# Attention probabilities split in fp16 halves and turned by a transposing DMA instead of TensorE

## Chip, core and metric

One NeuronCore of a Trainium2 chip runs the whole kernel as one program. The metric is the device time of one execution in microseconds (us). Engines: PE (TensorE: matmul and transpose into PSUM), DVE (VectorE), ACT (ScalarE), POOL (GpSimd), SP (SyncE, which here only issues DMAs). Each engine works through its own instructions in order and waits on semaphores.

## What is computed

One cross-attention layer and one FFN with 4-bit block quantisation, fp32 in and out. x is 2 x 1024 rows of 256, the context 2 x 154 rows of 256.

```python
# x = x + attention(layernorm(x), ctx, ctx);  16 heads of 64
q = einsum('bnd,hdk->bhnk', layernorm(x), proj_q) + bias_q
k = einsum('bnd,hdk->bhnk', ctx, proj_k) + bias_k
v = einsum('bnd,hdv->bhnv', ctx, proj_v) + bias_v
attn = softmax(q @ k.T / sqrt(64))            # rows of 154 per head
x = x + concat_heads(attn @ v) @ w_out.T
# x = x + ffn(layernorm(x));  fp4(.): blocks of 16, absolute maximum / 6 as scale, rounded to the grid 0 .. 6
h = silu(fp4(xn) @ fp4(w_gate).T) * (fp4(xn) @ fp4(w_up).T)     # 704 wide
x = x + fp4(h) @ fp4(w_down).T
```

## The kernel before

Every fp32 product is made of three fp16 matmuls: each operand is held as a high half and a low half (value minus high half), and `three` (L396) adds high x high, high x low and low x high in PSUM. The high half is made by ACT, the low half by DVE, as a rule out of PSUM.

After the loads and the keys, attention runs in 8 steps `i` of 256 rows (two tiles `s` of 128 rows). Sixteen heads are handled in four quads `j`, so there are 64 quads in all. For a quad, `score` (L522) puts 4 x 154 columns into two PSUM banks, `row_max` (L994, DVE) takes the maxima, `exps` (L742, ACT) the exponentials with their sums into `prob`, `inverse` (L1001, DVE) the reciprocal and `norm` (L1233, POOL) multiplies by it: the first 128 columns of each head in place, the other 26 into `rests`. The probabilities must then be turned, since the product with v sums over the 154 context rows. `turn_p` (L538, PE) transposes them as fp32 against the identity in five groups of four 128x128 blocks for each tile (four quads, and one group that gathers the rests), into one of two PSUM banks. `p_high` (L753, ACT) and `p_low` (L1005, DVE) write the halves of each group into `pT`, which has two buffers by step.

The four `heads` (L470) of step i-1, the four `query` parts (L507) of step i+1 and the projection `project` (L487) of step i-1 run among the groups of step i. Heads, the first values and the output weights share one PSUM bank (`O_BANK`, in the order `O_ORDER`, L253) with the projection, and query parts and the turned x another (`Q_BANK`). `add_attention` (L1010) adds the projection to x. In steps 1 to 6 a sixth of the FFN weights is quantised in passing: `block_scales` and `minus_grid` on DVE, `value` and a rounding product on POOL, an absolute value on ACT.

The body `attention` of each engine has ten groups a step (five to a tile), and runs the exponentials one tile ahead of the turning. The quantised FFN weights are turned (`turn_weights`, L547) in the last half step, when all exponentials are done. Then 16 FFN tiles follow (`ffn`), whose first four tiles also hold three of the four heads of step 7 and its projection. Stores are SP's only DMAs after the loads.

Of the kernel before, what the change touches and what calls it, by code (L numbers as in the profile page):

```python
# [33 lines left out]
CHUNKS = H + QUADS  # L34
GROUPS = QUADS + 1
# [6 lines left out]
W_STEPS = 6  # L42
WSLICE = WALL // W_STEPS

# [53 lines left out]
def xattn_ffn_kernel(nc, x, ctx_in, proj_q, bias_q, proj_k, bias_k, proj_v, bias_v, w_out,  # L98
                     w_gate, w_up, w_down, out):
    with ExitStack() as ctx:  # L100
# [16 lines left out]
        pT = sb("pT", [P, 2, 2, CHUNKS, 2 * P], F16)  # L117
# [22 lines left out]
        A2 = KC * W1 + FC * D + 2 * FP_ + 2 * FP_ + F + 6 * D  # L140
# [14 lines left out]
        bv = pT[0:1, 1].rearrange("p a c n -> p (a c n)")[:, 0:4 * H * DK].bitcast(F32)  # L155
# [4 lines left out]
        prob = arena[:, RAW:RAW + 2 * SC].rearrange("p (s n) -> p s n", s=2)  # L160
        REST0 = RAW + 2 * SC
        rests = arena[:, REST0:REST0 + 2 * H * RESTP].rearrange("p (s h n) -> p s h n", s=2, h=H)
        assert REST0 + 2 * H * RESTP <= 4 * RAW
# [15 lines left out]
        w1_h, w1_l = (take(KC * W1 // 2).bitcast(F16).rearrange("p (c n) -> p c n", c=KC) for _ in range(2))  # L179
        wdT = take(FC * D).bitcast(F16).rearrange("p (c n) -> p c n", c=FC)  # L180
        hq = take(2 * FP_).rearrange("p (s n) -> p s n", s=2)
        hT_h, hT_l = (take(FP_).bitcast(F16).rearrange("p (s n) -> p s n", s=2) for _ in range(2))
        silu = take(F)
# [4 lines left out]
        def over(n):  # L188
            mark[0] += n
            assert mark[0] <= 6 * RAW  # L190
            return arena[:, mark[0] - n:mark[0]]

        x_tmp = tuple(over(2 * D) for _ in range(3))
        assert mark[0] <= RAW + SC
        hid = over(2 * F).rearrange("p (s n) -> p s n", s=2)
        h_tmp = [tuple(over(F) for _ in range(3)), (over(F), wtmp[0], wtmp[1])]
        assert mark[0] <= 4 * RAW
        y = take(2 * D).rearrange("p (s n) -> p s n", s=2)
        xq = take(2 * D).rearrange("p (s n) -> p s n", s=2)
        xnorm = take(2 * D).rearrange("p (s n) -> p s n", s=2)  # L200
# [8 lines left out]
        T_BANK, O_BANK, Q_BANK = 4, 6, 7  # L209
# [14 lines left out]
        xn_ready, xt_mm, xt_high, xt_low = sem("xn_ready"), sem("xt_mm"), sem("xt_high"), sem("xt_low")  # L224
        q_mm, q_high, q_low = sem("q_mm"), sem("q_high"), sem("q_low")
        scored, max_done = sem("scored"), sem("max_done")
        exp_done, rinv_ready, normed = sem("exp_done"), sem("rinv_ready"), sem("normed")
        pt_mm, pt_high, pt_low = sem("pt_mm"), sem("pt_high"), sem("pt_low")
        o_mm, o_high, o_done = sem("o_mm"), sem("o_high"), sem("o_done")
# [4 lines left out]
        wt_mm, wt_high, wt_low, pad2_zero = sem("wt_mm"), sem("wt_high"), sem("wt_low"), sem("pad2_zero")  # L234
# [18 lines left out]
        O_ORDER = [("wo", n) for n in range(PAIRS // 2)]  # L253
        O_ORDER += [("v", b, n) for b in range(B) for n in range(3)]
        O_ORDER += [(kind, i, j) for i in range(STEPS) for kind, n in (("pv", QUADS), ("proj", 1)) for j in range(n)]
        O_AT = {j: n for n, j in enumerate(O_ORDER)}
        O_HIGH_AT = {j: n for n, j in enumerate(j for j in O_ORDER if j[0] != "proj")}
# [4 lines left out]
        def jobs_of(g):  # L262

            return range(W1_JOBS * g // GROUPS, W1_JOBS * (g + 1) // GROUPS)

        def down_jobs(s):

            return (range(W1_JOBS, len(WT_JOBS) - 1), range(len(WT_JOBS) - 1, len(WT_JOBS)))[s]

        def wt_bank(n):  # L270

            return n % 4 if n < W1_JOBS else HT_BANK + n % 2
# [15 lines left out]

        LAST_HEADS = (None, (0, 0), (0, 1), (1, 0))
        HEADS = ((0, 1), (0, 3), (1, 0), (1, 2))  # L290

        def queries(i):

            return ((0, 3), (0, 4), (1, 0), (1, 1)) if i == 0 else ((0, 0), (0, 2), (0, 4), (1, 1))

        def rows_in(i, s, g):

            if i == 0 and (s, g) == (0, 2): return 1
            return i + 2 if (s, g) == (1, 4) and exists(i + 2) else None

        def q_bank(i, j):

            return O_BANK + j % 2 if i == 0 else Q_BANK
# [18 lines left out]
        def last_quad(g):  # L322

            return min(QUADS - 1, g)

# [7 lines left out]
        def quad_T(part, i, s, g):  # L333

            return pT[:, i % 2, part, 4 * g:4 * g + 4, s * P:(s + 1) * P]

        def of_o(job):

            kind, a, j = job
            o = ps[:, O_BANK, :]  # L340
            if kind == "v":
                return o, v_h[:, a, j * 512:(j + 1) * 512], v_l[:, a, j * 512:(j + 1) * 512]
            return o, both(hidT_h[:, 2 * j:2 * j + 2]), both(hidT_l[:, 2 * j:2 * j + 2])
# [7 lines left out]
        def _(sp):  # L351
# [29 lines left out]
            sp.dma_start(wd_tiles, w_down.rearrange("(r p) f -> p r f", p=P)).then_inc(ld_ffn, 16)  # L381

# [12 lines left out]
        def _(pe):  # L395
# [34 lines left out]
            def next_o(job):  # L430

                wait(pe, o_done, O_AT[job])
                return ps[:, O_BANK, :]

            def turn_o(n):
                if n == 0: pe.wait_ge(ld_o, 16)
                wo = raw["o"].rearrange("p (r n) -> p r n", r=KC)
                o = next_o(("wo", n))
# [4 lines left out]
                last.then_inc(o_mm, 1)  # L443

            def values(b, n):
                o = next_o(("v", b, n))
# [4 lines left out]
                pe.matmul(o, ones[:, :], bv_l[:, n * 512:(n + 1) * 512], start=False, stop=True).then_inc(o_mm, 1)  # L451

            def rest_values(b):
                o = next_o(("v", b, 2))[:, 0:QUADS * DK].rearrange("p (a k) -> p a k", a=QUADS)
# [13 lines left out]
                last.then_inc(o_mm, 1)  # L468

            def heads(i, j):  # L470

                b = batch(i)
                if j == 0: pe.wait_ge(pt_low, GROUPS * (2 * i + 2))
                o = next_o(("pv", i, j))
                parts = ((v_h, vl_h, 0), (v_l, vl_l, 0), (v_h, vl_h, 1))
                for k in range(2):
                    for n, (vh, vr, part) in enumerate(parts):
                        for u in range(2):
                            h = 4 * j + 2 * k + u
                            pe.matmul(o[u * DK:(u + 1) * DK, k * 256:(k + 1) * 256], vh[:, b, h * DK:(h + 1) * DK],  # L480
                                      pT[:, i % 2, part, h], start=n == 0, stop=False)
                        for u in range(2):
                            last = pe.matmul(o[u * DK:(u + 1) * DK, k * 256:(k + 1) * 256], vr[:, b, j, 2 * k + u],
                                             pT[:, i % 2, part, H + j], start=False, stop=n == 2)
                last.then_inc(o_mm, 1)

            def project(i, part):  # L487
                if part == 0:
                    pe.wait_ge(o_done, O_AT[("pv", i, QUADS - 1)] + 1)
                    next_o(("proj", i, 0))  # L490
                todo = [(s, p) for s in range(2) for p in range(PAIRS)]
                for s, p in todo[16 * part // 3:16 * (part + 1) // 3]:
                    last = three(ps[:, O_BANK, s * D:(s + 1) * D], hidT_h[:, p, s * P:(s + 1) * P],
                                 hidT_l[:, p, s * P:(s + 1) * P], wot_h[:, p], wot_l[:, p], p == 0, p == PAIRS - 1)
                if part == 2: last.then_inc(o_mm, 1)

            def turn_x(i):

                pe.wait_ge(xn_ready, i + 1)
                wait(pe, q_low, QUADS * i)  # L500
                v = xn.rearrange("p s (d c) -> p s c d", c=KC)
                for c in range(KC):
                    for s in range(B):
                        last = pe.transpose(ps[:, Q_BANK, (2 * c + s) * P:(2 * c + s + 1) * P], v[:, s, c], ident[:, :])
                last.then_inc(xt_mm, 1)

            def query(i, j):  # L507

                if j == 0:
                    pe.wait_ge(xt_low, i + 1)  # L510
                elif q_bank(i, j) == q_bank(i, j - 1):
                    pe.wait_ge(q_low, QUADS * i + j)
                else:
                    wait(pe, q_low, j - 1)
                for k in range(2):
                    p = 2 * j + k
                    for c in range(KC):
                        last = three(ps[:, q_bank(i, j), k * 256:(k + 1) * 256], wq_h[:, c, p * P:(p + 1) * P],
                                     wq_l[:, c, p * P:(p + 1) * P], xnT_h[:, c], xnT_l[:, c], c == 0, c == KC - 1)
                last.then_inc(q_mm, 1)  # L520

            def score(i, s, j):  # L522


                n = QUADS * (2 * i + s) + j
                if s == 0:
                    pe.wait_ge(q_low, QUADS * i + j + 1)
                wait(pe, exp_done, n - 1)
# [9 lines left out]
            def turn_p(i, s, g):  # L538
                pe.wait_ge(normed, QUADS * (2 * i + s) + last_quad(g) + 1)
                wait(pe, pt_low, GROUPS * (2 * i + s) + g - 1)  # L540
                for k in range(4):
                    h = 4 * g + k
                    v = prob[:, s, h * L:h * L + P] if g < QUADS else rests[:, s, 4 * k:4 * k + 4].rearrange("p h n -> p (h n)")
# [3 lines left out]
            def turn_weights(jobs):  # L547

                for n in jobs:
                    kind, c, j0 = WT_JOBS[n]  # L550
                    if n == 0:
                        pe.wait_ge(wq_done, W_STEPS)
# [770 lines left out]
```

## Time and profile before

| | us |
|---|---|
| median of 3 runs | 435.87 |
| lowest and highest of the runs | 433.01, 435.90 |
| span of the profiled execution, first to last instruction | 431.8 |
| one attention step in the middle, by the repeat of the chain | 28.54 |
| first `hidden` (L1148) of the FFN | at 287.90 |

The profile is of one execution. Its busy times count an engine as busy while any instruction runs; matmuls overlap, and so do ACT's instructions, so a group's count times its mean can exceed its busy time. The chain of waits is followed back from the last instruction; its pieces show which engine ended each stretch. The span leaves out what lies before the first and after the last instruction, so it is compared with a run only roughly.

### The profile page before, as it was taken

Reading aid. Unit: us, or ns where it says so; the run is one execution under the profiler, and the core shown is the slowest. Engines: PE = TensorE matmul, PEld = TensorE weight load, DVE = VectorE, ACT = ScalarE, POOL = GpSimd, SP = SyncE. Lnnn points to the kernel's source line nnn. Section 1 sums busy time; section 2 is a strip of 40 time slices with the busy share of each in tenths; the row PEclk is TensorE's granted clock in tenths of the full one; section 3 lists DMA queues with packets and bytes.
Section 4 is the critical chain, followed back from the end, with each engine's and each line's share of the span. In section 5 each row is a group of like instructions: output and inputs, shape, how many; then the busy total and the mean of one; then the engine's idle time right before and its main releaser. Section 6 shows DMA issues by size and latency. Waiting matters only on the chain.

```text
span 431.8 us, 9502 instructions
## 1 busy us (share of the span) xinstructions
PE 367.8 (85%) x3691; PEld 282.7 (65%) x3691; DVE 348.9 (81%) x676; ACT 276.8 (64%) x869; POOL 200.1 (46%) x235
## 2 busy tenths in 40 slices
PE   1864798999989989999899967988785999999985
PEld 1543664777868778778687755855563776777764
DVE  2989866996988969879889798569779799999692
ACT  4766979887997897879978775365142255433331
POOL 3455313354454543544545544026643657676710
PEclk9998699999999999999999997999899799999999
DMA  7970000000000000000000000000000000000001
GB/s 218 322 275 1 2 2 0 5 2 0 4 2 2 0 4 2 1 2 4 2 2 2 2 1 2 0 2 2 1 2 13 14 20 18 14 24 14 24 27 36
DMA packets 8445, 11.48 MB, mean 27 GB/s; under 512 B 524, under 2 KB 6352, under 8 KB 8401
## 3 DMA queue, kind: packets, MB, share of 16 engines
q1 hardware_dynamic: 8401, 10.88, 8.0%
q8 instruction: 29, 0.48, 0.5%
q14 instruction: 15, 0.12, 0.1%
HBM read 8.78 MB, written 2.10 MB: 25 GB/s over the span
## 4 chain that ended last, share of the span: by engine, by line
DVE 38%; ACT 28%; PE 28%; issue 3%; DMA 1%; POOL 0%; SPq 0%; DVEq 0%; ACTq 0%
ACT arena L747 14%; PE ps L398 7%; PE ps L400 7%; PE ps L399 7%; ACT arena L738 5%; ACT pT L756 4%; DVE arena L1058 4%; DVE negmax L998 4%; DVE arena L1056 3%; DVE arena L989 3%; DVE arena L1182 2%; DVE pT L1007 2%; PE ps L544 2%; DVE blk_h L1023 2%; DVE arena L1148 2%
## 5 line engine op out<-in xcount | busy, mean ns | idle before, releaser
L747 ACT ACTIVATE arena<-ps,negmax 128x154 f32<-128x154 f32 x256 | 98.4, 430 | 16.1 <-DVE negmax L998 16.0
L1238 POOL TENSOR_TENSOR arena<-arena,rinv 128x104 f32<-128x104 f32 x64 | 23.1, 361 | 114.9 <-DVE rinv L1003 114.9
L1239 POOL TENSOR_TENSOR arena<-arena,rinv 128x512 f32<-128x512 f32 x64 | 66.7, 1042 | 0.0
L1007 DVE TENSOR_TENSOR pT<-ps,pT 128x512 f16<-128x512 f32 x80 | 54.6, 682 | 13.0 <-ACT pT L756 13.0
L747 ACT ACTIVATION_READ_ACCUMULATOR arena<-ps,negmax 128x1 f32 x256 | 63.4, 248 | 0.0
L544 PE MATMUL ps<-ident,arena 128*128 128x128 f32 x320 | 53.7, 292 | 4.0 <-DVE pT L1007 4.0
L756 ACT ACTIVATE pT<-ps 128x512 f16<-128x512 f32 x80 | 51.5, 644 | 5.5 <-PE ps L544 5.4
L998 DVE TENSOR_REDUCE negmax<-ps 128x4 f32<-128x616 f32 x64 | 50.2, 785 | 0.3 <-PE ps L534 0.2
L534 PE MATMUL ps<-kT_h,arena 64*128 64x154 f16 x512 | 37.8, 233 | 12.7 <-ACT arena L747 12.0
L398 PE MATMUL ps<-arena,xnT_h 128*128 128x352 f16 x128 | 40.8, 319 | 8.5 <-DVE xnT_l L1066 6.7
L544 PEld LDWEIGHTS ps<-ident,arena 128*128 128x128 f32 x320 | 35.2, 145 | 14.9 <-issue 7.9
L398 PE MATMUL ps<-arena 128*128 128x256 f16 (+2 forms) x120 | 35.6, 297 | 8.0 <-DVE arena L902 5.8
L534 PEld LDWEIGHTS ps<-kT_h,arena 64*128 64x128 f16 x512 | 23.2, 95 | 26.8 <-issue 17.1
L400 PE MATMUL ps<-arena,xnT_l 128*128 128x352 f16 x128 | 40.8, 318 | 0.0
L399 PE MATMUL ps<-arena,xnT_h 128*128 128x352 f16 x128 | 40.7, 318 | 0.0
L839 ACT ACTIVATE arena<-ps 128x704 f32<-128x704 f32 x16 | 12.1, 757 | 43.3 <-PE ps L400 43.3
L738 ACT ACTIVATE arena<-ps,biasT 128x256 f16<-128x256 f32 x64 | 27.6, 498 | 17.4 <-PE ps L400 17.4
L398 PE MATMUL ps<-wot_h,arena 128*128 128x256 f16 x128 | 34.9, 272 | 3.9 <-DVE arena L960 3.9
L398 PE MATMUL ps<-xnT_h,wq_h 128*128 128x256 f16 x128 | 35.0, 274 | 3.1 <-POOL wq_l L1230 1.7
L480 PE MATMUL ps<-pT,v_h 128*64 128x256 f16 x256 | 35.0, 283 | 1.2 <-DVE xs L1014 1.2
L399 PE MATMUL ps<-arena 128*128 128x256 f16 (+2 forms) x120 | 35.5, 296 | 0.0
L400 PE MATMUL ps<-arena 128*128 128x256 f16 (+2 forms) x120 | 35.5, 295 | 0.0
(153 smaller groups left out, 1039.3 us busy)
## 6 DMA issues: line engine op xcount, KB each, us to landing
out_dram<-arena SPq DMA_DIRECT2D x16, 128.0 KB, 1.7
xs<-in_x_dram SPq DMA_DIRECT2D x2, 512.0 KB, 7.3
arena<-in_L_xattn_w_out_dram SPq DMA_DIRECT2D x1, 1024.0 KB, 11.9
xs<-in_x_dram SPq DMA_DIRECT2D x2, 384.0 KB, 6.7
wffn<-in_L_ffn_w_down_dram SPq DMA_DIRECT2D x1, 704.0 KB, 9.3
wffn<-in_L_ffn_w_gate_dram SPq DMA_DIRECT2D x1, 640.0 KB, 7.7
wffn<-in_L_ffn_w_up_dram SPq DMA_DIRECT2D x1, 640.0 KB, 8.3
arena<-in_ctx_dram SPq DMA_DIRECT2D x1, 308.0 KB
```

Source lines behind the costliest of these rows:

```text
L398: pe.matmul(o, a_h, b_h, start=start, stop=False)
L399: pe.matmul(o, a_h, b_l, start=False, stop=False)
L400: return pe.matmul(o, a_l, b_h, start=False, stop=stop)
L480: pe.matmul(o[u * DK:(u + 1) * DK, k * 256:(k + 1) * 256], vh[:, b, h * DK:(h + 1) * DK], pT[:, i % 2, part, h], start=n == 0, stop=False)
L534: last = pe.matmul(ps[:, 2 * (j % 2) + u, k * L:(k + 1) * L], q[r, p, s * P:(s + 1) * P], kt[r, batch(i), p], start=n == 0, stop=n == 2)
L544: last = pe.transpose(ps[:, T_BANK + (s + g) % 2, k * P:(k + 1) * P], v, ident[:, :])
L738: last = act.activation(q_h[:, 2 * j + k], ps[:, q_bank(i, j), k * 256:(k + 1) * 256], ACT.Identity, bias=biasT[:, 2 * j + k:2 * j + k + 1])
L747: last = act.activation(prob[:, s, h * L:(h + 1) * L], ps[:, 2 * (j % 2) + k % 2, (k // 2) * L:(k // 2 + 1) * L], ACT.Exp, bias=negmax[:, ...
L756: act.activation(quad_T(0, i, s, g), ps[:, T_BANK + (s + g) % 2, :].rearrange("p (c n) -> p c n", c=4), ACT.Copy).then_inc(pt_high, 1)
L998: dve.tensor_reduce(negmax[:, s, 4 * j:4 * j + 4].rearrange("p (k u) -> p u k", k=2), v, AX.X, ALU.max, negate=True).then_inc(max_done, 1)
L1007: dve.tensor_tensor(quad_T(1, i, s, g), ps[:, T_BANK + (s + g) % 2, :].rearrange("p (c n) -> p c n", c=4), quad_T(0, i, s, g), ALU.subtrac ...
L1239: pool.tensor_tensor(v[:, :, 0:P], v[:, :, 0:P], r.to_broadcast([P, 4, P]), ALU.mult).then_inc(normed, 1)
```

## The change

`turn_p`, `p_high` and `p_low` out of PSUM go. POOL's `norm` writes the normalised quad to a new tile `normal` of 5 x 128 columns (four heads of 128, and the four rests of 26 padded to 32 each). `high_p` copies it to fp16, on ACT for odd quads and on DVE for even ones; `low_p` subtracts, on DVE for three quads of eight and on POOL for five. Both halves stand side by side in `split` (four buffers, one per quad `j`), and one transposing DMA per quad, issued by SP, turns all ten 128x128 blocks of it into `pT`. The loops of all engines become 64 slots, one per quad, with `score`, maximum and exponentials of quad n, `norm` of n-1 and the halves of n-2. Everything else that goes through PSUM (turned x, query parts, heads, values, output and FFN weights) becomes a task with a place in one order, `TASKS`, over three banks instead of two. The projection gets a bank of its own and is done by one pair of heads in each slot. The turns of the gate and up weights move into slots 57 to 62, next to the last exponentials; `layernorm` for the FFN covers five steps first and three later, instead of six and two. `prob` has one buffer per quad instead of two tiles. The heads of step 7 come in the first two FFN tiles, its projection in tiles 1 to 3.

```diff
+        def heads_at(i, j):
+            return 8 * (i + 1) + (2, 3, 5, 7)[j]
+        def query_at(i, j):
+            return 8 * (i - 1) + ((5, 6, 7, 8) if i == 1 else (4, 6, 8, 9))[j]
+        def wt_at(n):
+            return (57, 57, 60, 60, 62, 62)[n]
+        def task_bank(n):
+            if n == 0: return 7
+            if n <= QUADS: return 6 + (n - 1) % 2
+            return (4, 5, 7)[n % 3] if n < BODY else 4 + n % 2
+        def high_by_act(n):
+            return n % 2 == 1
+        def low_by_dve(n):
+            return n % 8 in (2, 5, 6)
...
+            def turn_p(n):                                   # SP
+                i, s, j = place(n)
+                wait_low(sp, n)
+                if i == 1: sp.wait_ge(task_mm, TASK_AT[VALUES[-1]] + 1)
+                if i >= 2: sp.wait_ge(task_mm, TASK_AT[("h", i - 2, j)] + 1)
+                sp.dma_start_transpose(pT[:, i % 2, j, :, :, s * P:(s + 1) * P].rearrange("p a c n -> p (a c) n"),
+                                       split[:, j]).then_inc(turned[j], 16)
...
+            for n in range(SLOTS):                           # PE
+                score(n)
+                if parts_of(n): project(*parts_of(n))
+                for t in tasks_of(n):
+                    task(t)
...
+            def high_p(n):                                   # ACT; DVE has the same with tensor_copy
+                j = n % QUADS
+                act.wait_ge(normed, n + 1)
+                wait(act, turned[j], 16 * (n // QUADS))
+                act.activation(part_of(j, 0), normal[:, j], ACT.Copy).then_inc(high_act, 1)
...
+            def slot(n):                                     # DVE, without the FFN's parts
+                row_max(n)
+                if n >= 1: inverse(n - 1)
+                if n >= 2 and not high_by_act(n - 2): high_p(n - 2)
+                if n >= 1:
+                    for t in tasks_of(n - 1):
+                        low(t)
+                if n >= 2 and low_by_dve(n - 2): low_p(n - 2)
+                if i == 0: first(n)
+                if m == 3 and i >= 2: add_attention(i - 2)
...
+            def low_p(n):                                    # POOL; DVE has the same
+                j = n % QUADS
+                wait_high(pool, n)
+                pool.tensor_tensor(part_of(j, 1), normal[:, j], part_of(j, 0), ALU.subtract).then_inc(low_pool, 1)
...
-            def turn_p(i, s, g):                             # PE
-                pe.wait_ge(normed, QUADS * (2 * i + s) + last_quad(g) + 1)
-                wait(pe, pt_low, GROUPS * (2 * i + s) + g - 1)
-                for k in range(4):
...
-                    last = pe.transpose(ps[:, T_BANK + (s + g) % 2, k * P:(k + 1) * P], v, ident[:, :])
-                last.then_inc(pt_mm, 1)
```

## Rows read from the trace of the kernel before

**Rows 1.** The page's first part: busy time, share of the span, instructions.

```profile
span 431.8 us, 9502 instructions
PE 367.8 (85%) x3691; PEld 282.7 (65%) x3691; DVE 348.9 (81%) x676; ACT 276.8 (64%) x869; POOL 200.1 (46%) x235
```

**Rows 2.** Windows: from:to and length, then busy us of each engine.

```profile
core 0: us, PE busy (x) PEld busy (x) DVE busy (x) ACT busy (x) POOL busy (x), PEclk, DMA share, GB/s
137.24:165.78 28.54, 26.85 (x334) 21.89 (x332) 23.88 (x47) 24.20 (x91) 13.87 (x19) 1.00 0.01 2
```

**Rows 3.** Chain of waits in that step: start us, us, engine and line.

```profile
138.72 0.49 ACT pT L756
139.70 1.49 ACT arena L747 x8
157.99 0.44 PE ps L544 x4
161.04 0.59 PE ps L544 x4
```

**Rows 4.** Single lines: durations min/median/max in ns; then groups: busy us, mean ns.

```profile
L1007 DVE TENSOR_TENSOR pT<-ps,pT x80: 628/691/693, 43.6 to 274.7; 128x512 f16<-128x512 f32 x80
L998 DVE TENSOR_REDUCE negmax<-ps 128x4 f32<-128x616 f32 x64 | 50.2, 785 | 0.3 <-PE ps L534 0.2
L955 DVE TENSOR_TENSOR vl_l<-ps,vl_h 26x256 f16<-26x256 f32 x8 | 3.4, 420 | 1.3 <-ACT vl_h L728 1.2
```

**Rows 5.** Groups by shape: nearest rows to the new operations out of SBUF.

```profile
L1230 POOL TENSOR_TENSOR arena<-arena 128x1024 f16<-128x1024 f32 x2 | 4.2, 2126 | 2.3 <-ACT arena L683 2.3
L777 ACT ACTIVATE arena<-arena 128x704 f32<-128x704 f32 x15 | 11.8, 786 | 0.0
L782 ACT ACTIVATE arena<-arena 128x512 f32<-128x512 f32 x8 | 5.0, 630 | 2.6 <-POOL arena L1246 2.6
L1177 DVE TENSOR_TENSOR arena<-arena 128x704 f32<-128x704 f32 x1 | 0.9, 893 | 0.0
L1174 DVE TENSOR_SCALAR arena<-arena 128x704 f32<-128x704 f32 x1 | 0.5, 527 | 0.0
L907 DVE BATCH_NORM_STATS2 stats<-xs 128x6 f32<-128x256 f32 x32 | 11.7, 414 | 0.3
```

**Rows 6.** Timelines of DVE and POOL (start us, us), and a line's undisturbed duration.

```profile
260.75 1.04 POOL L1239 TENSOR_TENSOR arena<-arena,rinv 128x512 f32<-128x512 f32 x1
260.93 0.88 DVE L938 SCALAR_TENSOR_TENSOR ln<-ln 128x12 f32<-128x12 f32 x1
261.85 0.17 DVE L939 TENSOR_TENSOR ln<-ln 128x12 f32<-128x12 f32 x1
...
297.61 2.23 POOL L1246 TENSOR_TENSOR arena<-arena,blk_h 128x704 f32<-128x704 f32 x1
297.71 0.87 DVE L1056 SCALAR_TENSOR_TENSOR arena<-arena 128x704 f32<-128x704 f32 x1
298.62 1.96 DVE L1058 SCALAR_TENSOR_TENSOR arena<-arena 128x704 f32<-128x704 f32 x1
...
L1246 POOL TENSOR_TENSOR arena<-wffn,blk_w x6: 1385/1387/1389, 91.9 to 234.6; 128x704 f32<-128x704 f32 x6
```

**Rows 7.** Windows of L747 alone (ACT busy, records); then of DVE's layernorm tile.

```profile
80.00:251.40 171.40, 80.31 (x392) 1.00 0.01 2
251.40:262.00 10.60, 4.78 (x24) 1.00 0.01 2
...
30.00:47.00 17.00, 5.57 (x19) 1.10 (x2) 0.78 0.00 0
251.00:262.50 11.50, 4.84 (x19) 0.03 (x1) 1.00 0.01 2
```

**Rows 8.** Chain of waits from the last exponential to the FFN.

```profile
260.17 0.18 DVE rinv L1003
287.90 0.81 DVE arena L1148
```

**Rows 9.** The page: GB/s in 40 slices; a DMA issue, KB, us to landing.

```profile
GB/s 218 322 275 1 2 2 0 5 2 0 4 2 2 0 4 2 1 2 4 2 2 2 2 1 2 0 2 2 1 2 13 14 20 18 14 24 14 24 27 36
out_dram<-arena SPq DMA_DIRECT2D x16, 128.0 KB, 1.7
```

More of the change, by code:

```diff
@@ L589, in first_o, with task @@
+            def task(t):
+                if t[0] == "x": turn_x(t[1])
+                if t[0] == "q": query(t[1], t[2])
+                if t[0] == "h": heads(t[1], t[2])
+                if t[0] == "w": turn_weights(t[1])
+                if t[0] == "wo": turn_o(t[1])
+                if t[0] == "v":
+                    if t == VALUES[0]:
                         pe.wait_ge(w_low, 3)
@@ new lines, in weights_high @@
+            def weights_high(n):
+                kind, c, j0 = WT_JOBS[n]
+                o = task_out(("w", n))
+                if kind == "w1":
+                    w = min(4, W1T - j0) * P
+                    last = act.activation(w1_h[:, c, j0 * P:j0 * P + w], o[:, 0:w], ACT.Copy, scale=-FS)
+                else:
+                    act.wait_ge(pad2_zero, 1)
+                    for k in range(2):
+                        m = min(P, F - (j0 + k) * P)
+                        last = act.activation(wdT[0:m, j0 + k, 0:D], o[0:m, k * D:(k + 1) * D], ACT.Copy, scale=-FS)
+                last.then_inc(task_high, 1)
@@ L831, in _ @@
+            act.wait_ge(w_scaled, 1)
+            split_part("v", wv_h, 1.0, 0)
+            high(("q", 0, 0))
+            split_part("v", wv_h, 1.0, 1)
+            for j in range(1, QUADS):
+                high(("q", 0, j))
             act.activation(unused[:, 0:1], biasT[:, 0:1], ACT.Exp)
-            for j in range(QUADS):
-                exps(0, 0, j)
             act.wait_ge(pad_zero, 3)
-            steps(act, attention)
+            for n in range(SLOTS):
+                slot(n)
+            if high_by_act(SLOTS - 2): high_p(SLOTS - 2)
@@ L1106, in stats_of @@
+            low(("x", 0))
             def stats_of(i):
@@ L1277, in _, with slot @@
-            steps(pool, attention, last=W_STEPS)
-            value_x(0)
+            def slot(n):
+                i, m = divmod(n, 8)
+                w = i - 1 if 0 < i <= W_STEPS else None
+                if n >= 1: norm(n - 1)
+                if n >= 2 and not low_by_dve(n - 2): low_p(n - 2)
+                if n == 16:
+                    pool.wait_ge(task_mm, TASK_AT[VALUES[-1]] + 1)
+                    pool.memset(wdT[:, FC - 1, :].bitcast(F32), 0.0).then_inc(pad2_zero, 1)
+                if w is not None:
+                    if m == 2:
+                        value(wtmp[0], wffn[:, w * WSLICE:(w + 1) * WSLICE], [blk_w[:, r] for r in range(4)],
+                              wscaled, wlowered, wvalued, w)
+                    if m == 7:
+                        pool.wait_ge(wgrid, w + 1)
+                        pool.tensor_tensor(blocks(wffn[:, w * WSLICE:(w + 1) * WSLICE]), blocks(wtmp[0]), spread(blk_w[:, 1]),
+                                           ALU.mult).then_inc(wq_done, 1)
+                if n == 60: value_x(0)
@@ L1279, in _ @@
+            for n in range(SLOTS):
+                slot(n)
+            norm(SLOTS - 1)
+            for n in (SLOTS - 2, SLOTS - 1):
+                if not low_by_dve(n): low_p(n)
             round_x(0)
```

665 lines of the change are left out of this document (312 added, 353 removed).

## The prediction

> **What bounds the kernel now.** I read the page's shares first: TensorE is busy for 85% of a span of 431.8 us [rows 1]. An average over stages says little, so next the windows: in one attention step of 28.54 us TensorE has 26.85, ACT 24.20, DVE 23.88 and POOL 13.87 us of work [rows 2]. The reader should see three engines near the limit and one half empty. The chain of waits inside that step hands over between them: ACT's exponentials (1.49 us for a quad of heads) and its copy of turned probabilities (0.49) in the first half, TensorE's matmuls and transposes (0.44 to 0.59 for four) in the second [rows 3]. Last the count of exponentials by window: 392 + 24 records after 80 us, eight to a quad, so 52 of 64 quads remain at 80 us. The last ends just before the reciprocal at 260.17, and the first FFN product (L1148) comes at 287.90, 27.7 us later, after turns, copies and projections that stand alone there [rows 7, 8]. So there are three things to gain: the first 80 us, the period, and that 27.7 us.
>
> **The change, part by part.** All per step of eight slots.
>
> *TensorE* loses ten groups of four fp32 transposes, about 0.5 us each [rows 3]: 26.85 - 5 = 21.9 us. Heads, queries and projection are the same matmuls, spread one task and one pair to a slot.
>
> *ACT* loses ten copies of 0.49 [rows 3] and gains four high halves of 128x640 from SBUF. The row for 704 is 0.786 and for 512 0.630 [rows 5], so 0.73: 24.2 - 4.9 + 2.9 = 22.2 us.
>
> *DVE* loses ten low halves of 0.68 [rows 4]. It gains four copies of 640 (one-source SBUF op, 704 in 0.527 [rows 5], so 0.49) and three subtractions of 640 (704 in 0.893 [rows 5], so 0.82): 23.9 - 6.8 + 2.0 + 2.5 = 21.6 us.
>
> *POOL* keeps its normalisation and gains five subtractions of 640. POOL's own fp32-minus-fp16 row has 1024 in 2.126 [rows 5], so 1.33: 13.9 + 6.6 = 20.5 us.
>
> By busy time alone all four engines come to 20.5 to 22.2 us. Before, period over the busiest engine was 28.54/26.85 = 1.06, which would make 23.5 to 24.5 us.
>
> *But DVE and POOL do not run freely beside each other.* At 260.93 DVE starts an operation on 12 columns that needs 0.17 us elsewhere and takes 0.88: it ends at 261.81, with POOL's 1.04 us multiplication from 260.75. At 297.61 POOL's 704-wide multiplication takes 2.23 us instead of 1.39, and DVE's from 298.62 takes 1.96 instead of 0.89 [rows 6]. The three there need 0.87 + 0.89 (another 704-wide one of two inputs, [rows 5]) + 1.39 = 3.15 us and get 2.97 from first start to last end: they ran in turn. Operations of DVE that read PSUM show no such stretch: the 80 low halves stay at 0.68 [rows 4]. The change takes DVE's second reading from PSUM to SBUF and gives POOL a second one as well. Work that excludes itself per step: POOL 20.5, DVE's halves 4.5, its two FFN-weight operations 1.8, in all 26.8 us. A period cannot be much shorter if the copies are excluded too, and 24.8 if they are not (no row shows a copy beside POOL). DVE is in order, so each of its nine such operations waits for what POOL has running: POOL is on for about three quarters of the time with operations of about 1.1 us, so some 0.45 us each, 4 us a step, and DVE stands at 21.6 + 4 = 25.6 before any hand-over. With 1.06 for hand-overs that is 27.2; I take 27.5, with 24.5 and 30 as ends.
>
> The Trainium skill (SBUF — State Buffer, Who interferes with whom) states this as an exclusive lock for a whole operation: DVE takes it with two SBUF inputs or in its fast copy mode, POOL whenever it reads SBUF. The rows above agree for two inputs; by the rule the copies are locked as well, the 26.8 case.
>
> *The DMA* turns 128x1280 fp16, 327,680 bytes, once a slot. No row shows a transposing DMA. From below: the loads moved 322 GB/s in the second slice, so 1.02 us. From above: ten 128x128 blocks, each as slow as a 128 KB store from issue to landing, 1.7 us [rows 9], in turn: 17 us. I take the first end plus one landing, about 2.7 us, since a store of similar form streams its rows in one landing. SP issues it alone and has nothing else to do before the first store. It is covered: by 3.4 us of slot for its rate, and by about four slots between the low half (slot n+2) and the heads (n+6) for its latency. Without that cover heads wait, then projection, then the buffer of four quads, which stalls the high halves.
>
> *Start and step 0.* Slot 0's maximum follows the last query half, so about 31.5 us. DVE in slots 0 to 7: eight maxima of 0.785, reciprocals 1.4, value halves 4x0.68 + 8x0.42, one turned x and one output-weight half 1.4, two query parts 1.9, six statistics 2.5, normalisation steps 5.6 [rows 4, 5, 7], probability halves 3.1: 28 us, with waits for POOL 29.5. Slots 0 to 7 end at 61; before, 12 quads stood at 80 us, now 61 + 5.5 slots of 3.44, so 13.5. Worth 5 us.
>
> *Steps 1 to 6:* 6 x 27.5 = 165, to 226. *Step 7* has the weights' turns and a normalisation with 19 dependent small operations; on DVE maxima 6.3, reciprocals 1.4, halves 4.4, head halves 2.7, weight halves 3.8, add and statistics 1.5, normalisation 4.8 [rows 7], x quantisation 2.8: 27.7, with waits for POOL 30.5. Last exponential at 257.
>
> *Tail.* The weights' turns and most of the projection are done in slots. From the last exponential: reciprocal and normalisation 1.6, high half 0.7, POOL's low half 1.3, rounding x 1.1, two turns and halves 1.6, four projection pairs 2.6, gate and up 3.6, silu 0.8, hand-overs 0.8: 14 us, to 271, against 287.9. The last DMA has those 14 us as cover. Two head tasks move into each of the first two FFN tiles, where three and the projection stood before: I leave the rest of 143.9 us as it is.
>
> *Sum:* 271 + 143.9 = 415 for a span of 431.8, a gain of 17. The median of the runs shown is 435.87 with 433.01 the lowest, so 1 to 4 us lie around the span; with 2, **417 us**. Where it goes: start 5, last exponential earlier by 3 in all (steps 1 to 6 gain, step 7 gives back), tail 14.
>
> **Rivals.** *The engines do not collide:* period 24.5 and no added waits in steps 0 and 7: 417 - 18 - 4 = 395. For it: the four busy sums; against it: the rows of operations in turn.
>
> *The DMA sets the pace* (the other side). A transfer of T us binds from 3.4 us on; the last exponential then stands at about 41 + 60T and the time at that + 160. It is level with before at T = 3.9 us (84 GB/s), 2% slower at 4.05, and at 17 us the time is 1,220. For it: nothing shows this kind of transfer. Against it: plain ones reach 322 GB/s. The Trainium skill gives both sides. VectorE: DVE Perf Modes (The three transpose paths) has 1.309 us for one 128x128 block against 0.390 on TensorE; ten in turn would be 13 us, and 41 + 60x13 + 160 = 980, an estimate. DMA: Bandwidth & Descriptors (Latency and other measured facts) has 261 GB/s for a transposing DMA, so 1.26 us, and the change would stand. No run here shows either.
>
> *Nothing gained in the steps:* waits for POOL add up along the in-order queues to a period of 30 to 30.5, 417 + 15 to 18 = 432 to 435: the same. For it: DVE's wait is on the way of every maximum, hence of every exponential.
>
> **How the numbers follow.** Forecast (period 26 to 29) 0.48, 406 to 427; no collisions 0.20, 390 to 403; DMA-paced 0.22, of which a quarter below 450; nothing gained 0.10. From 390 to 445 holds 0.48 + 0.20 + 0.10 + 0.03, about 8 in 10. One per cent is about what a measurement of this kernel can tell from no change. Faster: 0.48 + 0.20, less a little: 0.67. Same: 0.10. Slower: 0.23.
>
> **What would show it.** Right: attention periods of 26 to 29 us with DVE's 640-wide halves well above 0.49 and 0.82 on average, POOL's above 1.33, a DMA under 3.4 us a slot, and 14 us from last exponential to first L1148's counterpart. Wrong: periods of 24 with those at their bare durations; or SP's transfers back to back, with high halves waiting for them.

## The result and the profile after

The changed kernel takes 431.44 us (median of 11 runs, 429.8 to 432.14) against 434.68 for the kernel before beside it: a ratio of 0.9927, 95% interval [0.99, 0.9953]. That is 0.7% faster, inside the 1% that the prediction called no change, where it had put 417 us. Its chances stood on faster (0.67), with 0.10 on this outcome. The span went from 431.8 to 427.9 us.

The page's first part, to be held against [rows 1]:

```profile
span 427.9 us, 9077 instructions
PE 337.4 (79%) x3371; PEld 250.3 (58%) x3371; DVE 363.5 (85%) x652; ACT 259.6 (61%) x821; POOL 273.2 (64%) x275
```

The work moved as planned: TensorE lost 30 us, ACT 17, POOL gained 73. DVE, which was to lose 2.3 us a step by its bare operations, *gained* 15 in all and is now the busiest engine. Windows by the prediction's own terms (from:to and length, then busy us of each engine), cut at the maxima of slots 0, 8, 48 and 56, at 267.90, where the last record of the exponentials starts, and at the first FFN product (L1204 here):

```profile
31.67:67.21 35.54, 25.52 (x241) 13.41 (x242) 25.30 (x65) 24.16 (x90) 15.40 (x18) 0.81 0.24 47
67.21:205.64 138.43, 114.30 (x1450) 89.23 (x1450) 130.06 (x219) 110.83 (x420) 113.88 (x120) 0.95 0.52 94
205.64:239.73 34.09, 25.35 (x311) 19.42 (x311) 32.80 (x60) 22.77 (x87) 25.50 (x26) 0.91 0.49 91
239.73:267.90 28.17, 22.02 (x239) 16.41 (x237) 23.17 (x48) 21.93 (x84) 19.45 (x22) 0.80 0.41 79
267.90:288.70 20.80, 11.98 (x100) 8.83 (x100) 8.83 (x17) 6.74 (x14) 7.47 (x8) 0.75 0.33 64
288.70:427.90 139.20, 121.79 (x916) 91.19 (x912) 122.30 (x193) 55.51 (x103) 77.43 (x65) 0.99 0.05 16
```

| term | forecast | measured |
|---|---|---|
| maximum of slot 0 | 31.5 | 31.7 |
| slots 0 to 7 (step 0) | 29.5 | 35.5 |
| steps 1 to 5 | 5 x 27.5 = 137.5 | 138.4 |
| step 6 | 27.5 | 34.1 |
| step 7, to the last exponential | 30.5 | 28.2 |
| tail, to the first FFN product | 14 | 20.8 |
| the rest of the FFN | 143.9 | 139.2 |

The measured terms add up to 427.9. The period of a plain step was right to 1%; three terms of some 6 to 7 us each were not. Read against before, by the last record of the exponentials (first before, then after; start us, us):

```profile
259.59 0.21 ACT L747 ACTIVATION_READ_ACCUMULATOR arena<-ps,negmax 128x1 f32 x1
267.90 0.29 ACT L805 ACTIVATION_READ_ACCUMULATOR arena<-ps,negmax 128x1 f32 x1
```

The exponentials end 8.4 us *later* (268.2 for 259.8), and what follows them is 12.3 us shorter (159.7 for 172.0).

### The profile page after: what moved, and what is told of

Same layout as the page of the kernel before. It is cut to its first block, busy times and chain, and to the rows that moved or that the text cites. A ratio compares the mean times of both kernels' runs of the same rounds, so it can differ in the third digit from the quotient of the medians.

```text
span 427.9 us, 9077 instructions
## 1 busy us (share of the span) xinstructions
PE 337.4 (79%) x3371; PEld 250.3 (58%) x3371; DVE 363.5 (85%) x652; ACT 259.6 (61%) x821; POOL 273.2 (64%) x275
## 2 busy tenths in 40 slices
DMA packets 92413, 32.44 MB, mean 76 GB/s; under 512 B 84492, under 2 KB 90320, under 8 KB 92369
## 4 chain that ended last, share of the span: by engine, by line
DVE 58%; PE 18%; POOL 14%; issue 5%; ACT 3%; DMA 1%; SPq 0%; DVEq 0%; POOLq 0%
DVE negmax L1036 6%; POOL arena L1304 5%; POOL arena L1298 5%; DVE arena L1049 5%; DVE arena L1055 4%; DVE arena L1112 4%; DVE arena L1114 4%; DVE arena L998 3%; PE ps L456 3%; PE ps L458 3%; PE ps L591 3%; PE ps L457 3%; DVE arena L1027 3%; DVE arena L1238 3%; DVE blk_h L1069 2%
## 5 line engine op out<-in xcount | busy, mean ns | idle before, releaser
L805 ACT ACTIVATE arena<-ps,negmax 128x154 f32<-128x154 f32 x256 | 96.5, 395 | 46.8 <-DVE negmax L1036 46.5
L1297 POOL TENSOR_TENSOR arena<-arena,rinv 128x104 f32<-128x104 f32 x64 | 30.1, 470 | 64.5 <-DVE rinv L1042 64.5
L1298 POOL TENSOR_TENSOR arena<-arena,rinv 128x512 f32<-128x512 f32 x64 | 70.5, 1102 | 0.0
L1304 POOL TENSOR_TENSOR arena<-arena 128x640 f16<-128x640 f32 x40 | 63.7, 1592 | 0.8 <-ACT arena L816 0.8
L591 PE MATMUL ps<-kT_h,arena 64*128 64x154 f16 x512 | 39.8, 241 | 28.6 <-DVE arena L1027 18.7
L805 ACT ACTIVATION_READ_ACCUMULATOR arena<-ps,negmax 128x1 f32 x256 | 53.8, 210 | 0.0
L554 PE MATMUL ps<-wot_h,arena 128*128 128x256 f16 x128 | 37.8, 295 | 1.0 <-DVE arena L998 0.3
L555 PE MATMUL ps<-wot_l,arena 128*128 128x256 f16 x128 | 37.5, 293 | 0.0
L556 PE MATMUL ps<-wot_h,arena 128*128 128x256 f16 x128 | 37.4, 292 | 0.0
L457 PE MATMUL ps<-xnT_l,wq_h 128*128 128x256 f16 x128 | 36.3, 283 | 0.0
L458 PE MATMUL ps<-xnT_h,wq_l 128*128 128x256 f16 x128 | 36.2, 283 | 0.0
```

The source lines that it names most:

```text
L457: pe.matmul(o, a_h, b_l, start=False, stop=False)
L458: return pe.matmul(o, a_l, b_h, start=False, stop=stop)
L554: pe.matmul(o, a_h, wot_h[:, p], start=p == 0 and s == 0, stop=False, skip_group_check=True)
L555: pe.matmul(o, a_h, wot_l[:, p], start=False, stop=False, skip_group_check=True)
L556: last = pe.matmul(o, a_l, wot_h[:, p], start=False, stop=p == PAIRS - 1, skip_group_check=True)
L591: last = pe.matmul(ps[:, 2 * (j % 2) + u, k * L:(k + 1) * L], q[r, p, s * P:(s + 1) * P], kt[r, batch(i), p], start=n == 0, stop=n == 2)
```

## Experiments

Line numbers are those of the changed kernel (L1049 DVE's copy to fp16, L1055 DVE's and L1304 POOL's subtraction); kernels with an added line show them one higher. "Relative" means counted from the maximum of slot 0, since loading varies by 2 us from run to run.

**1. Is step 0 long because TensorE stands behind the turned x?** In the trace of after TensorE starts the turn of x for step 1 (L566) after 5.73 us of idling, and the chain to it runs through DVE's normalisation. Rows of the timeline there (start us, us; in brackets the idle time and its releaser):

```profile
41.72 1.39 POOL L1304 TENSOR_TENSOR arena<-arena 128x640 f16<-128x640 f32 x1
41.82 1.32 DVE L974 TENSOR_TENSOR ln<-ln 128x14 f32<-128x14 f32 x1
...
43.17 0.17 DVE L975 SCALAR_TENSOR_TENSOR ln<-ln 128x14 f32<-128x14 f32 x1
43.38 0.17 DVE L977 SCALAR_TENSOR_TENSOR ln<-ln 128x14 f32<-128x14 f32 x1
...
43.59 1.09 ACT L830 ACTIVATE arena<-xs,ln 128x256 f32<-128x256 f32 x2 [0.48 <-DVE ln L977]
...
44.74 1.13 PE L566 MATMUL ps<-ident,arena 128*128 128x128 f32 x4 [5.73 <-ACT arena L830]
...
45.66 0.63 PE L456 MATMUL ps<-arena 128*128 128x512 f16 x1
```

A 14-column operation waits for POOL's subtraction (1.32 us instead of 0.17), and the value products queued behind L566 then run one every 0.43 us, at a granted clock of 0.50 from 44 to 50 us (the lower of its two levels, 1.2 of 2.4 GHz). The experiment puts the values and output weights ahead of the turned x in each slot's tasks:

```diff
-            out = [("x", i) for i in range(1, STEPS) if rows_at(i) == n]
+            out = []
             if n < len(VALUES): out.append(VALUES[n])
             elif n < len(VALUES) + len(WOUT): out.append(WOUT[n - len(VALUES)])
+            out += [("x", i) for i in range(1, STEPS) if rows_at(i) == n]
```

> The changed kernel, with one order turned: in slot 3 the value task comes before the turned x. In the changed kernel TensorE stands for 5.7 us in front of the turned x of step 1, whose rows hang on DVE's normalisation chain, and then runs its values at the lower clock to 53 us; slots 0 to 7 take 35.5 us. Theory, TensorE blocked at the head of its queue: it does the values meanwhile, slots 0 to 7 take about 31.5 us and the kernel 4 us less than the changed one. Rival, DVE's own sum of work sets these slots: 35 us again, no change in time.

Measured: 426.69 us, ratio 0.9844 [0.9793, 0.9894], just below the interval of the changed kernel. Slots 0 to 7 take 31.98 us instead of 35.54, and the last exponential comes 3.8 us earlier, relative. So 3.6 us of the 6 are TensorE's queue behind the late x. The remaining 2.5 stay unexplained; DVE is busy for 25.3 us here too, and stands for 6.0 us in front of TensorE's scores, where it stood for 9.5 in after.

**2. Does POOL's reading slow DVE, or only POOL's presence?** POOL's subtractions of steps 0 to 5 become two fills of about the same length in all (0.95 + 0.36 us instead of 1.39). DVE's and ACT's instructions stay.

```diff
-    pool.tensor_tensor(part_of(j, 1), normal[:, j], part_of(j, 0), ALU.subtract).then_inc(low_pool, 1)
+    if n < 6 * 2 * QUADS:
...
+        pool.memset(arena[:, XN0:XN0 + 4 * D], 0.0)
+        pool.memset(part_of(j, 1).bitcast(F32), 0.0).then_inc(low_pool, 1)
+    else:
+        pool.tensor_tensor(part_of(j, 1), normal[:, j], part_of(j, 0), ALU.subtract).then_inc(low_pool, 1)
```

> The changed kernel, with POOL's five subtractions a step replaced, in steps 0 to 5, by two memsets of 1024 and 320 fp32 columns: about the same POOL time (0.94 + 0.36 us from such memsets elsewhere in the trace) but nothing read from SBUF. The low halves of these quads are zeros. Theory, DVE and POOL exclude each other when both read SBUF: DVE's subtraction of 640 falls from 1.15 us to near 0.82 on average, its copies from 0.93 towards 0.5 to 0.6 (they still meet the normalisation), and the step falls from 27.7 to 25 to 26 us. Rival, POOL's busy time and the in-order hand-overs set the period: durations of DVE fall little and the step stays above 27.2.

Measured: 422.81 us in one run, step 26.39. DVE's two operations, first in after, then here (min/median/max in ns over the run):

```profile
L1049 DVE CAST arena<-arena x32: 457/676/1675, 40.1 to 270.1; 128x640 f16<-128x640 f32 x32
L1055 DVE TENSOR_TENSOR arena<-arena x24: 806/1372/1443, 52.8 to 270.6; 128x640 f16<-128x640 f32 x24
```

```profile
L1049 DVE CAST arena<-arena x32: 454/464/1674, 40.1 to 263.0; 128x640 f16<-128x640 f32 x32
```

The lower median doesn't mean that a fill lets a copy pass: the copies of 0.46 us met no fill at all. Five copies of steps 0 to 5 did, and each of them ended 0.34 to 0.35 us after the second fill, whatever it had waited (0.85 to 1.50 us in all). Rows of DVE and POOL in this run, first one of these five, then the operation on `ln` that took 1.32 us in experiment 1:

```profile
134.50 0.95 POOL L1307 MEMSET arena<- 128x1024 f32 x1
134.75 1.34 DVE L1049 CAST arena<-arena 128x640 f16<-128x640 f32 x1
135.38 0.36 POOL L1308 MEMSET arena<- 128x320 f32 x1
...
41.68 0.95 POOL L1307 MEMSET arena<- 128x1024 f32 x1
41.80 0.17 DVE L974 TENSOR_TENSOR ln<-ln 128x14 f32<-128x14 f32 x1
```

So the answer differs by operation. One with two inputs in SBUF is held by a POOL that reads (1.32 us) and runs freely beside one that only fills (0.17). A copy is held by both, and so is DVE's one-source operation on 44 columns (L1071, 1.08 us beside the fills, 0.19 alone). The subtractions rise to 1.39 us (mean of the three in a step; 1.19 in after), since they now fall beside the normalisation, which still reads. The copies of the fourth step fall from 1.14 us on average to 0.78, because fewer of them meet POOL. The step falls by 1.3 us, between the two expectations; how much of this is the fills and how much the new timing was not separated. One more thing follows from the second pair of rows: although the hold of 1.15 us is gone, slots 0 to 7 take 35.56 us, as in after.

**3. Take DVE's copies away.** All high halves go to ACT (`high_by_act` returns True).

```diff
-            return n % 2 == 1
+            return True
```

> The changed kernel with all high halves on ACT, none on DVE. Theory, exclusion: four copies a step of 0.93 us leave DVE, work that excludes itself falls from 26.8 to 24.8 us and DVE's busy time from 26.6 to about 23; ACT rises from 22.2 to about 25. Step 25.5 to 26.5 us, kernel 5 to 10 us less. Rival, ACT becomes the bound with its waits for the maxima: step 27.5 or more, no gain.

Measured: 412.62 us, ratio 0.9519 [0.9476, 0.9562]. The window of one step, in after and here:

```profile
122.19:149.90 27.71, 23.24 (x292) 18.15 (x292) 26.66 (x45) 22.14 (x86) 23.21 (x25) 0.94 0.50 96
```

```profile
141.38:166.31 24.93, 21.91 (x295) 17.32 (x293) 22.99 (x41) 24.18 (x90) 23.42 (x25) 1.00 0.71 108
```

The step falls by 2.8 us and the kernel by 19, both more than expected. DVE loses 3.7 us of busy time, twice the bare price of four copies (4 x 0.46): half of what it had spent on them was waiting. ACT's busy time rises by 2.0.

**4. Reorder the tail.** In after, the chain of waits from the last exponential to the first FFN product has the longest pieces

```profile
270.80 1.59 POOL arena L1298
273.23 1.40 POOL arena L1304
274.62 1.02 POOL arena L1319
282.55 0.70 DVE xs L1060
284.02 0.60 DVE blk_x L1069
285.61 1.07 POOL arena L1311
287.37 0.70 DVE arena L1112
```

Ahead of them DVE rounds x (`grid_x(0)`, 267.83 to 270.04) before the last reciprocal; four pairs of the projection and the addition of step 6, with the scales of the next FFN tile, stand before the first product, which needs none of these. The experiment moves the rounding behind the reciprocal, and projection and addition into the first FFN tile (the last two pieces of the diff, for DVE and TensorE, stand in the loops over the FFN tiles):

```diff
-                if n == 63: grid_x(0)
...
             inverse(SLOTS - 1)
+            grid_x(0)
...
             xq_low(0, 0)
-            xq_low(0, 1)
-            add_attention(STEPS - 2)
             scales_x(1)
+            xq_low(0, 1)
...
+                    if (i, s) == (0, 0): add_attention(STEPS - 2)
...
-            for p in range(4, PAIRS):
-                project(STEPS - 2, p)
...
+                    if (i, s) == (0, 0):
+                        for p in range(4, PAIRS):
+                            project(STEPS - 2, p)
```

> The changed kernel with another order after the last exponential: DVE takes the last reciprocal before the rounding of x, the scales of the second x right after its first low half, and the addition of step 6 behind the first FFN tile's low halves; TensorE does the last four pairs of step 6's projection behind the first gate and up. Theory, the 20.8 us from last exponential to first FFN product are an order of work (reciprocal late by 2.1, projection at the lower clock 5, scales behind the addition): 14 to 16 us, of which 3 to 5 us are left at the end. Rival, given back: TensorE and DVE lack the time in the first FFN tiles, so the end moves by less than 1 us.

Measured: 431.52 us, ratio 0.9933 [0.9903, 0.9963]. The tail is 16.1 us (269.7 to 285.83) instead of 20.8, as expected, and nothing is won: relative to slot 0 the first product comes 4.8 us earlier, the second 0.3 and the last 0.8 us later. So all of the gain is lost between the first product and the second. This stretch in after, then here (busy us of PE, PEld, DVE, ACT, POOL):

```profile
288.70:296.80 8.10, 6.69 (x68) 5.02 (x66) 7.12 (x14) 3.55 (x10) 2.85 (x4) 1.00 0.01 2
```

```profile
285.83:298.99 13.16, 12.32 (x146) 9.83 (x144) 8.75 (x16) 5.07 (x12) 1.79 (x3) 1.00 0.00 1
```

It is TensorE that has no room to take the moved work in: it is busy for 12.32 of 13.16 us, DVE for 8.75. The chain of waits runs over the four pairs and the heads behind them on TensorE until 290.3, and only then over the addition and the scales on DVE.

**5. Does the DMA pace a step?** From step 2 on each transfer turns two of ten blocks (the rest of the probabilities stay those of earlier steps).

```diff
-                sp.dma_start_transpose(pT[:, i % 2, j, :, :, s * P:(s + 1) * P].rearrange("p a c n -> p (a c) n"),
-                                       split[:, j]).then_inc(turned[j], 16)
+                out, src = pT[:, i % 2, j, :, :, s * P:(s + 1) * P].rearrange("p a c n -> p (a c) n"), split[:, j]
+                if i >= 2: out, src = out[:, 0:2], src[:, 0:2 * P]
+                sp.dma_start_transpose(out, src).then_inc(turned[j], 16)
```

> The changed kernel, but from step 2 on the DMA turns two of the ten blocks of a quad (128x256 instead of 128x1280), so most of the turned probabilities are stale. Theory, the transfer is covered (SP stands waiting for low halves for 160 us in all): step 27.7, span within 2 us of the changed kernel's 427.9. Rival, the transfers (3.4 us from issue to landing) hold up heads or high halves: step below 27 and a span below 423.

Measured: 431.94 us in one run, with slot 0 two us later than in after; the step stays 27.7, though a transfer now lands in 2.3 us instead of 3.4 and moves a fifth of the bytes. The transfer is covered.

**6. Does the low clock of steps 6 and 7 cost time?** Granted clock falls to 0.78 in after from 226 to 240 us and to 0.50 from 247 to 254. The scores of slots 48 to 63 are computed twice, so that TensorE idles less.

```diff
-                for k in range(2):
+                for k in [*range(2)] * (2 if m >= 6 * 2 * QUADS else 1):
```

> The changed kernel, with every score of slots 48 to 63 computed twice over itself on TensorE: 16 times about 0.5 us at full clock of extra work. In the changed kernel the granted clock is 0.78 from 226 to 240 us, 0.74 to 247 and 0.50 to 254, and matmuls stand on the chain at 0.21 us each. Theory, the clock falls where TensorE idles, and its price there is about 3 us: the clock stays above 0.9 in slots 52 to 60 and the last exponential comes 2 to 3 us earlier. Rival, the extra work only costs: the same clock, or the last exponential later by up to 8 us.

Measured: 431.02 us in one run. The clock rises to 1.00 from 226 to 240 us, yet slots 48 to 55 take 34.06 us as before (34.09): the first four 0.4 us more, with the extra scores, the other four 0.4 us less. If the extra scores cost the second four as much as the first, the low clock there is worth about 0.8 us, where the theory had 3; DVE is busy for 32.8 of 34.1 us in after. From 247 to 254 the clock stays at 0.50, with 6.2 of 7 us busy in both, and the last exponential comes 1.4 us later, relative. What the low clock costs in step 7 this run can't show.

**7. Do experiments 1 and 3 add up?** Both edits together:

> Both edits that helped: the value task before the turned x in slot 3, and all high halves on ACT. If they act on different stretches (slots 0 to 7, and slots 8 to 63), the gains add: 412.6 minus 4 to 5, so about 408 us, slots 0 to 7 in 32 us and a step of 25. Rival, ACT, which then also carries slots 0 to 7, takes the gain of the first edit back: 411 or more.

Measured: 409.07 us, ratio 0.9411 [0.9369, 0.9452]. They add: 22.4 us less than the changed kernel, where the two gains make 23.6.

**8 and 9. Why is step 6 long?** It holds the normalisation for the FFN in slots 52 to 56: 19 small dependent operations on DVE. In kernel 7 (that of experiment 7) they read (DVE's timeline, the operations on `ln` alone, slots 53 and 54):

```profile
209.84 1.36 DVE L970 TENSOR_SCALAR ln<-ln 128x10 int32<-128x10 int32 x1
211.24 0.17 DVE L971 TENSOR_SCALAR ln<-ln 128x10 int32<-128x10 int32 x1
...
214.44 1.36 DVE L974 SCALAR_TENSOR_TENSOR ln<-ln 128x10 f32<-128x10 f32 x1
215.83 0.17 DVE L975 TENSOR_TENSOR ln<-ln 128x10 f32<-128x10 f32 x1
216.04 0.17 DVE L976 SCALAR_TENSOR_TENSOR ln<-ln 128x10 f32<-128x10 f32 x1
```

The first of each slot waits for POOL, 1.2 us; the others run at 0.17. Experiment 8 takes one Newton step (three operations) out of kernel 7:

```diff
-NEWTON = 3
+NEWTON = 2
```

> As the kernel before this one in the list, with two Newton steps instead of three in the four normalisation chains: three dependent DVE operations on up to 14 columns less in each, 0.17 us each when alone. Theory, each waits for what POOL has running, so they cost about 0.5 to 0.6 us each: the stretch of slots 52 to 55 falls by 1.5 to 2 us, slots 0 to 2 by 1, the kernel by 2 to 4. Rival, they cost their 0.17 us: the kernel falls by less than 1 us.

Measured: 409.04 us, ratio 0.9417 [0.9387, 0.9448], slots 52 to 55 in 19.23 us for 19.01. Relative to slot 0 the last FFN product comes 0.9 us earlier, so fewer operations bring less than 1 us: those taken out had no wait of their own, and the first operations of slots 53 to 55 still take 1.37, 1.36 and 1.35 us. Experiment 9 keeps all of them but puts them into one slot, so that only the first waits:

```diff
-                if 52 <= n < 57: layernorm(0, EARLY, 2 * LN_STEPS, [n - 52])
+                if n == 53: layernorm(0, EARLY, 2 * LN_STEPS)
```

> As the kernel with values first and all high halves on ACT, but all 19 dependent operations of the FFN's normalisation stand in slot 53 instead of five slots, 52 to 56. Theory (each slot's first operation of the chain waits once for POOL, 1.2 us, and the others follow at 0.17 to 0.2): four waits less, slots 52 to 56 take 15 to 17 us instead of 19.0, the time falls by 2 to 4 us to 405 to 407. Rival (the slots there are bound by the exclusive work as a whole, and a wait taken away comes back at the next operation): slots 52 to 56 at 18.5 to 19.5 us and 409.

Measured: 404.49 us, ratio 0.9338 [0.9304, 0.9372], the fastest of all. Its timeline, of POOL's one long operation and the start of the chain:

```profile
205.17 1.52 DVE L1132 SCALAR_TENSOR_TENSOR arena<-arena 128x704 f32<-128x704 f32 x1
205.91 2.05 POOL L1305 TENSOR_TENSOR arena<-arena 128x640 f16<-128x640 f32 x1
206.62 1.37 DVE L961 TENSOR_TENSOR ln<-stats 128x10 f32<-128x10 f32 x1
207.91 0.17 DVE L962 TENSOR_TENSOR ln<-stats 128x10 f32<-128x10 f32 x1
```

Here the two engines can be seen taking turns: POOL's subtraction starts at 205.91, but takes 2.05 us instead of 1.39, since DVE's product runs to 206.7; DVE's next operation, of ten columns, ends at 207.99, as POOL's does at 207.96. Eighteen more follow within 3.3 us. Slots 52 to 55 take 16.1 us for 19.0, and slots 52 to 62 36.9 for 41.8. Kernel 7 has four such waits (0.9, 1.2, 1.2, 1.2; slot 56 has none), here one is left: that makes 3.3 of the 4.8 us. Where the other 1.5 come from was not followed up. Against the kernel before beside each run, the gain over kernel 7 is 3.2 us (0.9338 for 0.9411), by the last FFN product relative to slot 0 it is 5.0.

**10. One more subtraction from POOL to DVE** (kernel 7, `low_by_dve` for four slots of eight).

```diff
-            return n % 8 in (2, 5, 6)
+            return n % 8 in (0, 2, 5, 6)
```

> As the kernel with values first and all high halves on ACT, but the low halves of four slots of eight on DVE instead of three. Theory (DVE's two-input operations and all of POOL share one path, 24.8 us of work in a period of 24.9): one subtraction at 0.82 in place of POOL's 1.39 takes 0.55 us of exclusive work away, period 24.3 to 24.5, time 3 to 5 us less, 404 to 406. Rival (ACT's own 24.2 us of a period of 24.9 bind now): period 24.8 to 25.0, 409. Second rival (DVE in order is next to bind, 23.0 busy + 0.82 + a wait of 0.5): 24.9 to 25.5, 409 to 412.

Measured: 409.56 us, ratio 0.9452 [0.9434, 0.947], period 25.13. The theory missed: exclusive work was to fall by 0.55 us, and the period rose by 0.2 from kernel 7's 24.9.

```profile
137.49:162.62 25.13, 21.79 (x294) 17.29 (x293) 24.04 (x42) 24.16 (x89) 22.08 (x24) 1.00 0.66 106
```

DVE and ACT both stand at 24 of 25.1 us, and DVE's subtractions rose from 1.12 us on average to 1.28. At a period of 25 the exclusive path no longer binds by itself. The period lies in the range of the second rival (DVE) and 0.13 us outside that of the first (ACT), which is too little to tell them apart.

## Why the prediction was right and wrong

Of a forecast gain of 17 us in the span, 3.9 came. The mechanism of the period was right; the steps that failed are three terms of the sum: step 0, summed on DVE alone; the normalisation before the FFN, put into the wrong step and priced as if it ran freely; and the tail, summed without regard to its order and to the FFN behind it.

*Slot 0 and the period:* right, 31.7 for 31.5 and 27.7 for 27.5, and for the reason given, though with some luck in the size. DVE's held operations in the step from 122.19 to 149.90 (count, busy us, mean ns; then the idle time):

```profile
L1049 DVE CAST arena<-arena 128x640 f16<-128x640 f32 x4 | 4.6, 1141 | 0.1
L1055 DVE TENSOR_TENSOR arena<-arena 128x640 f16<-128x640 f32 x4 | 4.4, 1090 | 0.0
L1131 DVE SCALAR_TENSOR_TENSOR arena<-arena 128x704 f32<-128x704 f32 x1 | 1.5, 1499 | 0.0
L1134 DVE SCALAR_TENSOR_TENSOR arena<-arena 128x704 f32<-128x704 f32 x1 | 1.4, 1442 | 0.0
L1071 DVE TENSOR_SCALAR blk_w<-blk_w 128x44 f32<-128x44 f32 x1 | 1.2, 1245 | 0.0
```

Alone they take 0.46, 0.81, 0.89 twice and 0.19 us. The last one was not among the forecast's nine places. DVE is busy for 26.66 us, so the waits come to about 5 us over the bare 21.6, where the forecast had 4 and 25.6 in all; the period is 1.04 times that instead of 1.06, and the two errors nearly cancel. The rival without collisions falls with these durations. The open half of the question, whether copies are held up as well, is answered: beside a POOL that reads they are (1.67 us), and beside one that only fills too (experiment 2). The section of the Trainium skill cited in the prediction (SBUF — State Buffer, Who interferes with whom) says that copies in DVE's fast mode contend with GpSimd, and operations with two SBUF inputs only with a GpSimd instruction that reads. The trace agrees in both: 1.34 us for a copy beside fills, 0.17 for the two-input operation beside a fill and 1.32 beside a subtraction.

*The DMA:* no pace. One transfer takes

```profile
pT<-arena SPq DMA_TRANSPOSE x64, 3.4
```

from issue to landing, 0.7 more than the estimate and exactly where the forecast would have had it bind if transfers could not overlap; but a 0.50 share of the DMA engines in a step means about 1.7 us of work a slot, and SP itself waits for the halves, not the reverse (SP's waits: us in total, times, longest):

```profile
SPq L435 <- POOL arena L1304: 122.3, 40, 21.1
SPq L435 <- DVE arena L1055: 38.5, 18, 5.0
```

Experiment 5 confirms it. Of the two figures of the Trainium skill in the prediction, 1.309 us per 128x128 bf16 block (VectorE: DVE Perf Modes, The three transpose paths) can't be added up over the ten blocks of one transfer, which land together in 3.4 us; 1.26 us, from 261 GB/s (DMA: Bandwidth & Descriptors, Latency and other measured facts), is below the 1.7 us of DMA work a slot.

*Step 0, +6 us:* what failed was to cost it by DVE alone. The forecast summed DVE's operations to 28 us; they are busy for 25.3 of 35.5. What sets the end is a chain over DVE, ACT and TensorE: the second normalisation, spread over slots 0 to 2, makes the turned x late, and everything queued behind it on TensorE waits (experiment 1, 3.6 us of it). That POOL holds one operation of it for 1.15 us is not the reason, since experiment 2 takes this hold away and slots 0 to 7 stay at 35.56. The other 2.5 us stay open.

*Step 6, +6.6, and step 7, -2.3:* the normalisation was put into the wrong step (it lies in slots 52 to 56, which are all but one in step 6), and its price was mis-sized: 4.8 us by busy time from [rows 7], as if each of the 19 operations ran freely. In after, 15 operations of it lie between the maxima of slots 52 and 56, at about 0.2 us each (3.0), with one wait of 1.2 in each of slots 53 to 55 (L969 1.37, L973 1.36 and 1.35 for a bare 0.17): 6.6 us. Experiment 9, made on kernel 7, takes most of the waits away and gets 4.6 us of time back (409.07 to 404.49). Step 6 then takes 29.2 us where a plain step takes 24.9; the 19 operations with their one wait lie between 206.62 and 211.21, 4.6 us.

*The tail, +6.8, and the FFN, -4.7:* the sum of 14 listed the operations and missed their order. `grid_x(0)` stands before the last reciprocal, and four projection pairs, the addition, the scales of the next tile and its rounding stand before the first product (278 to 288.7). Experiment 4 shows that as a term of the sum this was not worth 6.8 us: with the tail 4.7 us shorter, the FFN is 5.5 longer, since the four pairs then fill TensorE between the first two products. Tail and FFN belong together: 157.9 us forecast, 160.0 measured. So the real miss lies before the last exponential, 10.9 us late, and of that experiments 1 and 9 recover about 8.

*Where the gain went:* TensorE's and ACT's relief was real, and what follows the last exponential is 12.3 us shorter, but the halves came to lie on the pair DVE and POOL, which takes turns. By the starts of the maxima, eight quads at a time, the times before and after are 28.2 and 35.5, 33.2 and 27.3, then 28.5 and 27.7 (28.0 once) for steps 2 to 5, 28.5 and 34.1, and to the last exponential 25.1 and 28.5. So the steps in the middle gain 0.5 to 0.8 us each, steps 0 and 1 lose 1.4 together, step 6 loses 5.5 and step 7, which now has the turns of the gate and up weights and the last of the normalisation in it, 3.4. Moving four copies a step to ACT (18 to 19 us), one change of order in step 0 (4 to 5) and gathering the normalisation (3 to 5) nearly add up and make the same design 6.6% faster than before.

## What to carry to other kernels

When work is moved to POOL, budget POOL's operations on SBUF together with DVE's copies and two-input operations on SBUF as one resource (only the two-input ones passed a POOL that merely fills), and price DVE's waits by the number of places where it meets a running POOL operation, not by the size of its own: nineteen tiny operations in a row cost one wait, in five places four. Charge each piece of work to the slot in which the code issues it, and sum a start-up stage along the chain that crosses engines rather than on its busiest one. An early first result is no gain when the engine behind it is full: sum a tail together with the stage it runs into.

## What the hardware showed beyond the forecast

A transposing DMA within SBUF moves 327,680 bytes (ten fp16 blocks of 128x128) in 3.4 us from issue to landing, and two blocks in 2.3 us; SP's issue of one takes 1.45 us (at 43.14). The program has 92,413 DMA packets, of which 84,492 are under 512 bytes. DVE's one-source copy within SBUF is held up by a reading POOL (up to 1.68 us for a bare 0.46) and by a filling one (0.85 to 1.50 in all five cases); an operation with two SBUF inputs is held by the reading one (1.32 for 0.17) and was not held by the fill (0.17). A POOL operation that comes second waits too (2.05 us for 1.39). Step 6, with DVE 96% busy, took the same time when extra matmuls went with a granted clock of 1.00 over 14 us instead of 0.78.
